# One Perceiver block on one core: K projected straight into its transposed form, its norm applied as the scale of the exponentials

## The reference

```python
xn = layernorm(x, ln_x_g, ln_x_b)          # 4096 context rows of 256
ln = layernorm(latents, ln_l_g, ln_l_b)    # 256 latent rows of 256
q = (ln @ Wq)                              # 16 heads of 64
kv = jnp.concatenate([xn @ Wkv, ln @ Wkv], axis=1)
qn = rmsnorm(q, qn_g) * scale              # rmsnorm: x / max(norm(x) / 8, eps) * gamma, per head
kn = rmsnorm(k, kn_g)
sim = jnp.einsum('bhid,bhjd->bhij', qn, kn)
attn = jax.nn.softmax(sim, axis=-1)
out = jnp.einsum('bhij,bhjd->bhid', attn, v)
return out @ Wout + bout
```

## Time and profile before

| | us |
|---|---|
| median of 3 runs | 711.73 (711.15 to 712.97) |
| profiled execution, its own time | 711.47 |
| its span in the trace | 709.8 |
| periods of pass 0 in it | about 33 to 151 |
| periods of passes 1 to 3 | about 151 to 525 |
| last sums, Performer, experts | from about 525 |

### The profile page before, as it was taken

One profiled execution on the slowest core, in us unless ns is written; L12 is line 12 of the kernel. 1 busy time (PEld: TensorE's weight loads), 2 busy tenths in 40 slices (PEclk: granted clock), 3 DMA queues, 4 the chain that ended last, 5 costly groups with the idle time before them and its releaser, 6 DMA issues. The chain is left out here.

```text
span 709.8 us, 14199 instructions
## 1 busy us (share of the span) xinstructions
PE 650.6 (92%) x5054; PEld 518.6 (73%) x5054; DVE 493.5 (70%) x977; ACT 416.5 (59%) x878; POOL 238.0 (34%) x219
## 2 busy tenths in 40 slices
PE   1899999899999999999999999999984685999997
PEld 0777776677677777767777776777763674999997
DVE  2699898866867676686767668676765624676674
ACT  3688888656566566656666565566652302674651
POOL 3534434532223343222334322322210023345540
PEclk9999999999999999999999999999996856999999
DMA  5021450100000010000000000000003004256510
GB/s 159 30 61 31 127 175 1 46 1 2 1 16 16 2 31 1 2 1 16 2 1 1 2 1 1 16 2 1 2 1 118 0 1 156 85 178 211 165 36 16
DMA packets 26130, 30.49 MB, mean 43 GB/s; under 512 B 4169, under 2 KB 23762, under 8 KB 26066
## 3 DMA queue, kind: packets, MB, share of 16 engines
q1 hardware_dynamic: 23410, 28.79, 12.8%
q10 hardware_dynamic: 2656, 0.86, 0.5%
HBM read 29.38 MB, written 0.26 MB: 42 GB/s over the span
## 5 line engine op out<-in xcount | busy, mean ns | idle before, releaser
L783 POOL TENSOR_TENSOR k_rms<-k_ss,neg_half 128x4 f32<-128x4 f32 x136 | 136.9, 1007 | 313.8 <-DVE k_ss L676 313.8
L525 ACT ACTIVATE probs<-s_ps,minus_bound 128x512 f32<-128x512 f32 x272 | 164.4, 686 | 90.4 <-PE s_ps L379 90.4
L168 PE MATMUL kv_ps<-w_quad,xn 128*128 128x512 f32 x816 | 212.2, 407 | 1.9 <-issue 1.9
L670 DVE SCALAR_TENSOR_TENSOR probs_sum<-probs,tile_mask,probs_sum 128x512 f32<-128x512 f32 x264 | 192.3, 764 | 5.2 <-ACT probs L525 4.8
L168 PEld LDWEIGHTS kv_ps<-w_quad,xn 128*128 128x128 f32 x816 | 148.2, 189 | 45.7 <-issue 6.7
L392 PE MATMUL o_ps<-probs,v 128*64 128x256 f32 x1088 | 132.6, 385 | 0.8 <-ACT probs L525 0.7
L379 PEld LDWEIGHTS s_ps<-q_parts,kt 64*128 64x128 f32 x1632 | 101.1, 185 | 36.0 <-issue 20.0
L379 PE MATMUL s_ps<-q_parts,kt 64*128 64x256 f32 x1632 | 115.0, 287 | 9.2 <-DVE kt L680 9.2
L654 DVE SCALAR_TENSOR_TENSOR kn<-k_rms,kv_ps 128x256 f32<-128x256 f32 x136 | 56.6, 416 | 67.4 <-POOL k_rms L783 66.9
L392 PEld LDWEIGHTS o_ps<-probs,v 128*64 128x64 f32 x1088 | 72.0, 136 | 41.9 <-issue 10.8
L517 ACT ACTIVATE kt<-s_ps 128x256 fp32r<-128x256 f32 x136 | 44.8, 382 | 64.2 <-PE s_ps L365 64.1
(11 more groups left out here) (179 smaller groups left out, 624.4 us busy)
## 6 DMA issues: line engine op xcount, KB each, us to landing
w_raw<-in_ffn_W SPq DMA_DIRECT2D x18, 1024.0 KB, 5.4
rows<-in_ctx SPq DMA_DIRECT2D x8, 512.0 KB, 4.1
w_raw<-in_L_xattn_Wkv SPq DMA_DIRECT2D x6, 256.0 KB, 3.1
wout<-in_L_xattn_Wout SPq DMA_DIRECT2D x4, 256.0 KB, 2.7
wq_raw<-in_L_xattn_Wq SPq DMA_DIRECT2D x3, 256.0 KB, 4.6
w_raw<-in_L_xattn_Wkv ACTq DMA_DIRECT2D x2, 256.0 KB, 6.9
wq_raw<-in_L_xattn_Wq ACTq DMA_DIRECT2D x1, 256.0 KB, 4.1
x_res<-in_x SPq DMA_DIRECT2D x1, 256.0 KB, 3.7
```

The lines of the kernel that those rows point to most:

```text
L168: last = nc.tensor.matmul(out, stationary(k, s), moving(k, m), start=n == 0, stop=n == len(terms) - 1)
L525: nc.scalar.activation(probs[n % P_RING][:, :, c, :], s_ps[n % 2][c][:], ACT.Exp, bias=minus_bound[:]).then_inc(exp_done, 1)
L670: nc.vector.scalar_tensor_tensor(total, probs[n % P_RING][:, :, c, :], seen, total, ALU.mult, ALU.add).then_inc(sum_done, 1)
L783: nc.gpsimd.tensor_tensor(k_rms[n % 2][:].rearrange("p i c -> p (i c)"), k_ss[n % 2][:].rearrange("p i c -> p (i c)"), neg_half[:, 0:4], A ...
```

## The change

Only the attention block changes.

- `project(m)` makes a pair at once. K comes out transposed: the weights are the stationary operand and both tiles' `xn` the moving one (256 columns, two runs of 128), twelve matmuls into one bank `k_ps`; V as before per tile, but twelve matmuls of 256 columns into one bank `v_ps`. Both banks are single; project waits for `square` of the pair before (K) and for `keep_v` (V).
- `transpose_k` and `scale_k` are gone. `keep_kt` and `kt_rest` take 512 elements from `k_ps` a turn earlier than before; `square` follows `kt_rest`.
- `sum_squares(m)`: four plain fp32 products of the squares (stationary, 128x128) with two columns of ones per head pair, into eight columns of `s_ps[0][0]`; `keep_squares` on DVE copies them out with a floor; `scores` waits for that.
- `root` now stands in the turn in which the pair's scores are made, both roots of a pair in a row; its result is the scale of the exponentials, which are split by head pair: eight of 256 elements, with scale and bias from memory.
- On DVE the last `add_weights` of a turn moves ahead of `statistics`.
- `rows` has two buffers instead of three, and the loads of rows and of `wout` are re-ordered to suit; four memsets of `head_rows` are added at the start of DVE.

```diff
+            def project(m):
+                g, u = m // NU, m % NU
+                if u == 0:
+                    pe.wait_ge(w_lo, g + 1)
+                if g == 0:
+                    pe.wait_ge(xn_lo, u + 1)
+                if m:
+                    pe.wait_ge(sq_done, m)
+                for j in range(2):
+                    last = part_products(nc, k_ps[:, j, :], lambda k, s: w_quad[g % 2][:, k, s, j * P:(j + 1) * P],
+                                         lambda k, s: xn[:, 2 * u:2 * u + 2, k, s, :])
+                last.then_inc(k_done, 1)
+                if m:
+                    pe.wait_ge(v_kept, 2 * m)
+                for i in range(2):
+                    last = part_products(nc, v_ps[:, i, :], lambda k, s: xn[:, 2 * u + i, k, s, :],
+                                         lambda k, s: w_quad[g % 2][:, k, s, D:2 * D])
+                last.then_inc(v_done, 1)
...
+            def sum_squares(m):
+                pe.wait_ge(sq_done, m + 1)
+                if m:
+                    pe.wait_ge(exp_done, 4 * m - 3)
+                for i in range(2):
+                    for j in range(2):
+                        last = nc.tensor.matmul(ss_ps(i)[:, 2 * j:2 * j + 2], k_sq[m % 2][:, j, i * P:(i + 1) * P], head_rows[:],
+                                                start=True, stop=True)
+                last.then_inc(ss_done, 1)
...
             def scores(n):
                 g, b = n // NT, n % 2
-                pe.wait_ge(kt_lo, n - n % 2 + 2)
+                pe.wait_ge(kt_lo, n // 2 + 1)
+                pe.wait_ge(ss_kept, n // 2 + 1)
...
+            def square(m):
+
+                act.wait_ge(kt_lo, m + 1)
+                if m >= 2:
+                    act.wait_ge(ss_done, m - 1)
+                nc.scalar.activation(k_sq[m % 2][:], k_ps[:], ACT.Square, scale=DH ** -0.5).then_inc(sq_done, 1)
...
+                act.wait_ge(rms_done, n + 1)
                 for c in range(2):
                     act.wait_ge(s_done, 2 * n + 1 + c)
-                    nc.scalar.activation(probs[n % P_RING][:, :, c, :], s_ps[n % 2][c][:], ACT.Exp, bias=minus_bound[:]).then_inc(exp_done, 1)
+                    for j in range(2):
+                        last = nc.scalar.activation(probs[n % P_RING][:, j, c, :], s_ps[n % 2][c][:, j, :], ACT.Exp,
+                                                    scale=k_rms[n // 2 % 2][:, n % 2, 2 * j + c:2 * j + c + 1], bias=minus_bound[:])
+                    last.then_inc(exp_done, 1)
...
+            def keep_squares(m):
+                dve.wait_ge(ss_done, m + 1)
+                if m >= 2:
+                    dve.wait_ge(rms_done, 2 * (m - 1))
+                nc.vector.tensor_scalar_max(k_ss[m % 2][:].rearrange("p i h -> p (i h)"), s_ps[0][0][:, 0, 0:8], RMS_FLOOR ** 2).then_inc(ss_kept, 1)
```

More of the change, by code:

```diff
@@ L189, in attention @@
         gq_col, gqk_col = ring(1, "gq_col", [P, 2])[0], ring(1, "gqk_col", [P, 1])[0]
-        rows = ring(3, "rows", [P, GT, D])
+        rows = ring(2, "rows", [P, GT, D])
         stats, mean_var = ring(2, "stats", [P, 2, 6]), ring(2, "mean_var", [P, 2, 2])
@@ L213, in attention @@
         bout = ring(1, "bout", [P, D])[0]
-        kv_ps = [ctx.enter_context(nc.psum_tensor(f"kv_ps{b}", [P, 2, D], F32)) for b in range(2)]
+        k_ps, v_ps = [ctx.enter_context(nc.psum_tensor(name, [P, 2, D], F32)) for name in ("k_ps", "v_ps")]
         s_ps = [[ctx.enter_context(nc.psum_tensor(f"s_ps{h}{c}", [P, 2, NQ], F32)) for c in range(2)] for h in range(2)]
@@ L419, in _ @@
             project(0)
-            project(1)
             transpose_z(2)
@@ L497, in keep_qt, with keep_kt @@
                 nc.scalar.activation(q_parts[t % 2][:, :, 0, :], o_ps[t % 2][:], ACT.Copy, scale=gqk_col[:]).then_inc(qt_hi, 1)
-            def square(n):
-                act.wait_ge(kv_done, n + 1)
-                if n >= 2:
-                    act.wait_ge(ss_done, n - 1)
-                nc.scalar.activation(k_sq[n % 2][:].rearrange("p j c d -> p (j c d)"), kv_ps[n % 2][:, 0, :], ACT.Square,
-                                     scale=DH ** -0.5).then_inc(sq_done, 1)
+            def keep_kt(m):
+                act.wait_ge(k_done, m + 1)
+                if m >= 2:
+                    act.wait_ge(s_done, 4 * (m - 1))
+                nc.scalar.activation(kt[m % 2][:, 0], k_ps[:], ACT.Copy).then_inc(kt_hi, 1)
+            def square(m):
[3 more added lines that the diff above has]
+                nc.scalar.activation(k_sq[m % 2][:], k_ps[:], ACT.Square, scale=DH ** -0.5).then_inc(sq_done, 1)
             def keep_v(n):
+                act.wait_ge(v_done, n // 2 + 1)
                 if n >= V_RING:
@@ L545, in _ @@
             square_q(0)
-            square(0)
+            keep_kt(0)
             act.wait_ge(mask_done, 1)
             keep_v(0)
-            square(1)
             keep_v(1)
+            square(0)
             gain(2)
@@ L566, in _ @@
                 if exists(e + 2):
-                    square(e + 2)
-                for n in (e, e + 1):
-                    if exists(n):
-                        keep_kt(n)
-                if exists(e + 2):
+                    keep_kt(m + 1)
                     keep_v(e + 2)
-                    square(e + 3)
                     keep_v(e + 3)
+                    square(m + 1)
                 if m + 3 < NU:
@@ L694, in add_out @@
                 nc.vector.tensor_tensor(x_res[:], x_res[:], o_ps[g % 2][:], ALU.add).then_inc(y_added, 1)
+            for half in range(2):
+                for c in range(2):
+                    nc.vector.memset(head_rows[half * DH:(half + 1) * DH, c:c + 1], float(half == c)).then_inc(halves_done, 1)
             statistics(0)
@@ L824, in _ @@
             root_q(0)
-            root(0)
-            root(1)
             root_of(3)
```

132 lines of the change are left out of this document (44 added, 88 removed).

## The result

The changed kernel takes **742.27 us** in the median (742.09 to 743.81), the kernel before beside it 712.33. The ratio is 1.0423, with an interval of 1.0407 to 1.044: slower by 4.2%. Forecast were 734.3 us and a range of 722 to 745. Direction and range were right; of the 30.8 us between the two profiled executions (742.25 and 711.47) the sum had found 22.8. The profiled execution before is one of the quickest of its kernel: in the 44 executions of it beside the later runs, 31 have a mean granted clock of 0.959 and take 712.7 to 714.7 us, four have 0.966, as the profiled one, and take 710.9 to 711.5.

What follows compares the result with a forecast made beforehand. PE was taken to bound passes 1 to 3, a ring over other engines pass 0. Ring +9.6, next period -1.3, 54 other periods +18.9, stalls -3.6, start -0.8: +22.8 on 711.47, so 734.3 us; range 722 to 745 (78%).

Steps and rivals of the forecast that it cites:

- What bounds the kernel: Passes 1 to 3: only PE's own work counts, 6.93 us a period; pass 0: a ring over ACT, DVE and POOL.
- the ring: Pass 0: exponentials, K's rounding and rest, sum, statistics, root, offset, z; 8.4 us a turn, +9.6 us over twelve turns.
- Projection: PE: 24 matmuls of 256 columns instead of twelve of 512 cost nothing, 2.91 us against 2.90 a period.
- Sums of squares: PE: eight load-bound instructions at 0.11, 0.88 us, replace four transposes of 0.53; net +0.35 us a period.
- The rival of cheap products: PE's sum_squares phase takes 0.22 instead of 0.88 us, so the whole is faster, 698 us; chance 4%.
- Its threshold: The sum_squares phase, about 0.46 us, below which the changed kernel would be faster than the kernel before.
- The period behind it: Period after pass 0's twelve turns: 2.01 us wait for K's rest shrinks to about 0.4; net -1.3 us.
- Stalls: Waits around the changes of pass: those after the reciprocals go, those at new queries mostly stay; -3.6 us together.
- The reciprocals' stall: After passes 0, 1, 2 reciprocals delay kt_rest on DVE, holding scores up by 0.97 us; goes, -3.0 us.
- The queries' stall: Three stalls at a new pass's queries mostly stay, since qt_rest still precedes keep_squares on DVE; -0.6 us.
- Start: Beginning of the kernel: PE waits less for K, about -0.8 us.
- End: End of the attention: last exponentials 1.3 us longer, last waits for K gone; 0 in total.

Runs made afterwards that it cites:

- The wide and the unscaled exponentials: Changed kernel, exponentials without the key's norm as scale (computation partly left out): four of 512 elements, 726.73 us; eight of 256, 727.99 us.
- bf16: Changed kernel with the squares and the columns of ones in bfloat16 instead of fp32: 706.93 us, ratio 0.9898.
- the later splits: Changed kernel with POOL's two splits of the next queries' and K/V weights one turn later in pass 0: 740.74 us.
- the run with the rounding moved: Changed kernel with ACT's rounding of the next pass's transposed queries ahead of the turn's exponentials: 739.27 us, ratio 1.0365.
- the kernel before with the two edits: Kernel before with POOL's weight splits one turn later and the queries' rounding ahead of the exponentials: 710.05 us, ratio 0.996.
- early statistics: Changed kernel with DVE's statistics ahead of keep_squares and kt_rest, and POOL's root_of ahead of the two roots: 734.97 us.
- the best version: Changed kernel with bf16 squares, statistics earlier, POOL's splits later, queries' rounding before exponentials, ACT's square behind the rows' affine and xn: 686.8 us.

## Why the prediction was right, and by what it was short

**What bounds the kernel.** Right: PE in passes 1 to 3, the ring in pass 0. The wide and the unscaled exponentials left 7.32 alone, and the type of the short products moved it.

**Projection.** Right, shown by the halved matmuls alone. K's twelve take 0.11 more than V's, and that is the first load standing open and not the operand in two runs: in the kernel before with halved matmuls, whose operand is contiguous, the first ten take 1.27 us and the other fourteen 1.64, which leaves the same 0.10 at the front. For the two runs there remain at most the 0.03 by which 2.93 exceeds 2.90. That 0.03 over 52 periods is 1.6 of the missing 8.0 us.

**Sums of squares.** Right to 0.01 us, 0.88, by L970, a row with a like shape and type. The rival of cheap products came true only with another type. Its threshold, a phase of 0.46, came from a sum that was 8 us short: to win back 30.8 us in 54 periods the phase must fall by 0.57, to 0.31. Indeed 0.43 still gave 719 us, and 0.19 went below the kernel before. Its slope held by the periods: 54 x 0.46 is 25, measured 23; 54 x 0.71 is 38, measured 35. The query periods stayed at 8.36 to 8.38 in both, which kept back 1.4 and 2.1, and in bf16 the period behind pass 0 rose from 9.48 to 10.73, where the granted clock was 0.57 from 139 to 143 us. What was priced correctly as load-bound was not asked further: which type makes the load cheap.

**The ring.** Right link by link: eleven turns at 8.39, and the twelfth, with ACT's two weight roundings, at 9.83, make +9.8 for +9.6.

**The period behind it.** The failed step is "only keep_squares can be late". POOL's splits ran beside the offset and z, which lie on the ring, and stretched them to 1.25 and 2.53 us. So the period gave back 0.5 of the forecast 1.3; the later splits returned 1.09, which shows it.

**Stalls.** The reciprocals' stall went, and was worth more than the forecast 3.0: the two periods of 7.98 and 7.19 a pass are at 7.31, 3.9 us with the base taken off. The queries' stall grew by 0.1 each instead of shrinking by 0.2. The prediction followed DVE's order only and missed that ACT's rounding stands behind exponentials that are 1.3 us longer; the run with the rounding moved shows that this was all of it. The two misses balance. A rest of about 0.6 us lies in the periods with the queries' products (8.84 against 8.34) and was not looked into.

**Start.** -2.1 for -0.8, but 1.1 of it is no effect of the change. The first projection takes 4.38 us in the profile before (21.05 to 25.43) and 3.32 after (20.21 to 23.53); the same instructions as before take 3.44 in the kernel before with the two edits, and 2.91 with the matmuls halved. What sets its length in an execution stays open. About -1.0 is left, near the forecast.

**End.** The largest miss, 6.8 for 0.7, and the step was "last exponentials 1.3 longer, last waits for K gone: 0". They do not cancel. Up to the final sums 2.7 us are missing: PE waits 2.1 us more, and its last matmuls of the attention at the lower clock level take 0.6 more. Wide exponentials took back 3.0 of this way, so the cause of the waits is ACT. The 3.3 us from the sums on are 2.3 of difference between executions, as the runs above show, and 0.9 for the final sums at the lower level. With the 2.3 taken out, and the 1.1 of the start the other way, the profiles differ by 29.6 us by the change, and the sum lacked 6.8.

That PE's longer waits bring the lower clock at the sums is not shown. In the five profiles with 15.5 to 16.9 us from the last projection to the final sums these eight matmuls took 1.08 us; in the nine with 17.7 us or more they took 1.97 in six and 1.08 in three. So the long way goes with the lower level often, not always. It is alike elsewhere: behind a wait of 1 to 2 us near the end of pass 0 the clock fell in four profiles (halved matmuls, bf16, early statistics, queries first; 1.5 to 1.8 us each) and not in others with as long a wait. Six executions of the best version fell into three with a mean granted clock of 0.953 over the span (687.8 to 688.5 us) and three with 0.963 to 0.965 (683.1 to 685.8). What decides between them stays open.

## What to carry to other kernels

Ask of every short matmul what it pays for: with two columns the price is the weight load, times the instructions that the type makes of a product, and a type with a cheap load can turn the sign of a change. Where a ring sets the time, write down the start of each link, and look at which foreign instruction can fall beside one of them; the same split of weights cost 1.1 us on the changed kernel's ring and nothing a turn later. Before sizing the end of a stage, count the work of the last turn that nothing follows, and give an error of a few us to the clock: before explaining a difference of under 5 us between two profiles, compare the granted clock of both, stretch by stretch, and look for another execution of the same code.

## What was not expected of the hardware

- A 128x128 weight load with two moving columns behind it costs 0.11 us in fp32 and in fp32r, and 0.05 in bf16.
- An exponential of 256 elements costs its queue 0.358 us with one operand from memory and 0.449 with two.
- POOL's split of 1024 elements held a DVE instruction of 0.41 us for 2.53, to within 0.15 of the end of the split. In the other direction, a DVE sum beside it makes POOL's two-element `var_eps` last 0.62 instead of 0.22.
- One and the same program varies by 3 to 5 us with the mean granted clock: the kernel before took 710.9 to 711.5 us at 0.966 (four executions), 711.5 to 713.0 at 0.962 to 0.964 (eight), 712.7 to 714.7 at 0.959 (31) and 715.3 at 0.957 (one).
